# Expert rows gathered in tiles: the first product computed turned from copied weights, and a new order of work

## The reference

```python
x = x + L1_xcond(layernorm(x), ctx, ...)      # cross attention, 16 heads, layer 2 of the kernel
x = x + L1_ffn(layernorm(x), ...)             # layer 3, "sorted"
x = x + L2_xcond(ctx, layernorm(x), ...)      # local attention with a window, layer 4, "local"
...
# L1_ffn: 8 experts, each token goes to one
h = relu(einsum('td,edh->teh', tokens, W1) + b1[None])      # 128 -> 256
y = einsum('teh,ehd->ted', h, W2) + b2[None]                # 256 -> 128
out = take_along_axis(y, expert)[:, 0, :]; return out * max_prob
```

## Time and profile before

| | |
|---|---|
| runs, us | 961.96, 957.6, 962.65; median 961.96 |
| profiled execution | 961.87 us, span on the core 960.1 us |
| mean granted TensorE clock | 0.868 of full speed |
| busy share PE / DVE / ACT / POOL | 75% / 61% / 36% / 26% |
| chain that ended last | PE 48%, DVE 25%, POOL 8%, issue 8%, ACT 5%, DMA 4% |

### The profile page before, as it was taken

The page is one execution under the profiler, slowest core; times in us unless marked ns, Lnnn a source line. Parts: engine busy times, 40 slices in busy tenths (PEclk is TensorE's granted clock), DMA queues, the critical chain, the costliest instruction groups (busy, mean ns, idle before and its releaser), DMA issues.

```text
span 960.1 us, 13382 instructions
## 1 busy us (share of the span) xinstructions
PE 724.2 (75%) x3940; PEld 452.8 (47%) x3940; DVE 590.4 (61%) x2000; ACT 346.5 (36%) x582; POOL 254.2 (26%) x304
## 2 busy tenths in 40 slices
PE   2677874889984766675777459777867788789998
PEld 1223332889982222234656335655644233355554
DVE  6656647455455556553544558798777566586673
ACT  6255412645650552242121122122314456323221
POOL 2240267550664654112340431120111100000000
PEclk9979865899996895787987669979989899699999
DMA  6273022354643411611211000203011110000000
GB/s 177 62 249 112 17 77 91 118 174 133 189 135 85 112 48 30 204 70 53 81 46 42 23 0 1 74 1 80 1 50 50 50 50 1 0 1 12 12 12 11
DMA packets 71216, 65.65 MB, mean 68 GB/s; under 512 B 8996, under 2 KB 62941, under 8 KB 70634
## 3 DMA queue, kind: packets, MB, share of 16 engines
q1 hardware_dynamic: 53610, 48.14, 17.1%
q0 software_dynamic: 5120, 10.50, 3.7%
q10 hardware_dynamic: 12416, 6.16, 2.2%
HBM read 35.73 MB, written 22.94 MB: 61 GB/s over the span
## 4 chain that ended last, share of the span: by engine, by line
PE 48%; DVE 25%; POOL 8%; issue 8%; ACT 5%; DMA 4%; SPq 1%; DVEq 0%; ACTq 0%; POOLq 0%
PE psum_all L700 4%; PE psum_all L676 4%; DVE s_nmx L1340 4%; PE psum_all L678 3%; PE psum_all L805 3%; PE psum_all L893 3%; PE psum_all L657 3%; PE psum_all L787 3%; PE psum_all L789 3%; PE psum_all L909 2%; ACT s_hT L2102 2%; DVE s_x_normed L1237 2%; PE psum_all L775 2%; PE psum_all L613 2%; POOL routed_x L2426 2%
## 5 line engine op out<-in xcount | busy, mean ns | idle before, releaser
L2520 POOL TENSOR_SCALAR s_vare<-s_mv 128x4 f32<-128x4 f32 x40 | 11.6, 289 | 388.1 <-DVE s_mv L1229 378.8
L1340 DVE TENSOR_REDUCE s_nmx<-psum_all 128x4 f32<-128x308 f32 x192 | 83.2, 473 | 49.9 <-PE psum_all L657 46.3
L2102 ACT ACTIVATE s_hT<-psum_all 77x1024 f32<-77x1024 f32 x96 | 95.9, 1017 | 40.6 <-PE psum_all L678 40.5
L676 PE MATMUL psum_all<-s_t,s_ks 128*77 128x512 bf16 x192 | 84.1, 438 | 13.1 <-ACT s_hT L2102 9.6
L657 PE MATMUL psum_all<-s_ks,s_t 128*128 128x308 bf16 x192 | 59.6, 360 | 44.2 <-DVE s_nmx L1340 30.1
L678 PE MATMUL psum_all<-s_t,s_ks 128*77 128x512 bf16 x192 | 82.6, 430 | 0.0
L700 PE MATMUL psum_all<-s_hT,s_v 77*32 77x512 f32 x384 | 59.2, 690 | 26.1 <-ACT s_hT L2102 26.0
L2440 POOL DMA_INDIRECT s_w<-routed_y,s_cT x64 | 61.8, 966 | 56.1 <-issue 55.2
L2426 POOL DMA_INDIRECT routed_x<-s_x_normed,s_cT x64 | 62.4, 975 | 45.5 <-DVE s_cT L1541 27.2
L657 PEld LDWEIGHTS psum_all<-s_ks,s_t 128*128 128x128 bf16 x192 | 18.4, 103 | 99.1 <-DVE s_nmx L1340 65.8
L2199 ACT ACTIVATE s_hT<-psum_all,s_cols 128x128 f32<-128x128 f32 x188 | 51.1, 382 | 36.8 <-PE psum_all L893 32.7
(11 more groups left out here) (315 smaller groups left out, 1528.7 us busy)
## 6 DMA issues: line engine op xcount, KB each, us to landing
s_t<-q_parts SPq DMA_DIRECT2D x66, 128.0 KB, 2.9
routed_y<-s_hT ACTq DMA_DIRECT2D x22, 256.0 KB
s_ks<-s_att SPq DMA_DIRECT2D x72, 77.0 KB, 2.1
q_parts<-s_qparts SPq DMA_DIRECT2D x11, 384.0 KB, 2.3
s_arena<-in_w SPq DMA_DIRECT2D x2, 2048.0 KB, 10.7
s_h<-routed_x SPq DMA_DIRECT2D x48, 64.0 KB
s_x_normed<-routed_x SPq DMA_DIRECT2D x46, 64.0 KB
routed_x<-s_w SPq DMA_DIRECT2D x34, 64.0 KB, 1.5
```

The costliest lines, as they stand in the source:

```text
L676: pe.matmul(PS[0:SK, k + y, :], KS1[:, h, keys], T1[:, u % QS, h // HPG, :], start=True, stop=False)
L1340: read(job, dve.tensor_reduce(nmx[:, u % 2, i, HPG * g:HPG * g + HPG], PS[:, k, 0:HPG * SK].rearrange("p (h s) -> p h s", h=HPG), AX.X, AL ...
L2102: read(("S", L, b, p), nc.scalar.activation(Eexp[:, (PAIRS * u + p) % ES, :, :], PS[0:SK, k:k + 2, :], ACT.Exp))
```

## The change

- Inner rows turned: `sorted_hidden` on TensorE multiplies with a copy of the expert's W1 (`SW1`, in the place of `HSg`) as the stationary operand, so that its product comes out turned, in two halves of 128; there is no bias matmul. ScalarE adds the bias as a column (new columns `b1_3` in the table `cols`, chosen by a register) in eight ReLU activations a quad and writes `HTg` itself. `sorted_turn_hidden` and `sorted_copy` are gone.
- VectorE copies W1 of each tile (`sorted_first_weights`), ahead of the quad.
- `attn_out` of the last batch stands ahead of the tiles; the first two turnings of each half stand together; the values follow the next quad's inner rows; fronts, route, rank and local scores have new places; `local_add` of batches 0 and 1 moves from the end of the sorted layer into `local_layer`, behind `front_stats(L, 2)`.
- `PB` and its two helpers hold 128 columns instead of 384; `r_end` shares the memory of `tile_expert`.

TensorE:

```diff
             def sorted_hidden(L, h, q):
                 n = len(QUADS[L]) * h + q
                 have(("XT", L, h, q))
+                pe.wait_ge(s_rw1, R_STEPS + n + 1)
                 k = start(("SH", L, h, q), WIDE)
-                for i, t in enumerate(QUADS[L][q]):
-                    o = PS[:, k + i // 2, 256 * (i % 2):256 * (i % 2) + 256]
-                    pe.matmul(o, XST[:, n % 2, 128 * i:128 * i + 128], w1_rows[:, bass.ds(expert_at[h, t], 256)],
-                              start=True, stop=False)
-                    mm = pe.matmul(o, SEL[:, bass.ds(expert_at[h, t] // 2, 128)], PB[:, 0:256], start=False, stop=True)
+                for i in range(len(QUADS[L][q])):
+                    for c in range(2):
+                        a = 256 * i + 128 * c
+                        mm = pe.matmul(PS[:, k + a // 512, a % 512:a % 512 + 128], SW1[:, n % 2, a:a + 128],
+                                       XST[:, n % 2, 128 * i:128 * i + 128], start=True, stop=True)
                 finish(("SH", L, h, q), mm)
```

VectorE:

```diff
-            def sorted_copy(L, h, q):
...
+            def sorted_first_weights(L, h, q):
+
+                n, some = len(QUADS[L]) * h + q, QUADS[L][q]
                 if n >= 2:
-                    dve.wait_ge(*slots.is_made(("SY", L, (n - 2) // len(QUADS[L]), (n - 2) % len(QUADS[L]))))
...
+                    dve.wait_ge(*slots.is_made(("SH", L, (n - 2) // len(QUADS[L]), (n - 2) % len(QUADS[L]))))
+                dve.wait_ge(s_te, h + 1)
+                regs = r_regs[0:len(some)]
+                dve.reg_load(regs, tile_expert[0:1, h, some[0]:some[-1] + 1])
+                at = [dve.snap(r, min_val=0, max_val=(EXPERTS[L] - 1) * 256) for r in regs]
+                for i in range(len(some)):
+                    ins = dve.tensor_copy(SW1[:, n % 2, 256 * i:256 * i + 256],
+                                          w1[L][:, :, :].rearrange("p e h -> p (e h)")[:, bass.ds(at[i], 256)])
+                ins.then_inc(s_rw1, 1)
```

`local_layer` on VectorE, and ScalarE's inner rows:

```diff
                 sorted_add(L - 1, 1, range(0, TPB))
                 front_stats(L, 2)
+                local_add(L, 0)
+                local_add(L, 1)
                 front_stats(L + 1, 0)
                 front_apply(L, 2)
```

```diff
             def sorted_hidden(L, h, q):
-                n = len(QUADS[L]) * h + q
-                w = 256 * len(QUADS[L][q])
+                n, some = len(QUADS[L]) * h + q, QUADS[L][q]
                 k = made(("SH", L, h, q))
+                act.wait_ge(s_te, h + 1)
                 if n >= 2:
-                    act.wait_ge(*slots.is_made(("HT", L, (n - 2) // len(QUADS[L]), (n - 2) % len(QUADS[L]))))
-                read(("SH", L, h, q), nc.scalar.activation(HSg[:, n % 2, 0:w], PS[:, k:k + 2, :].rearrange("p a b -> p (a b)")[:, 0:w],
-                                                           ACT.Relu))
+                    act.wait_ge(*slots.is_made(("SY", L, (n - 2) // len(QUADS[L]), (n - 2) % len(QUADS[L]))))
+                regs = r_regs[0:len(some)]
+                act.reg_load(regs, tile_expert[0:1, h, some[0]:some[-1] + 1])
+                at = [act.snap(r, min_val=0, max_val=(EXPERTS[L] - 1) * 256) for r in regs]
+                first = COLS["b1_3"][0]
+                for i in range(len(some)):
+                    for c in range(2):
+                        a = 256 * i + 128 * c
+                        ins = nc.scalar.activation(HTg[:, n % 2, a:a + 128], PS[:, k + a // 512, a % 512:a % 512 + 128], ACT.Relu,
+                                                   bias=cols[:, first + c:first + 15 + c][:, bass.ds(at[i] // 128, 1)])
+                read(("SH", L, h, q), ins)
```

More of the change, by code:

```diff
@@ L1768, in sorted_layer @@
                 gauss_context()
[L1770 removed]
+                first(1, 2)
+                values(1, 0)
                 sorted_add(L, 0, range(0, TPB))
                 front_stats(L + 1, 0)
+                first(1, 3)
+                values(1, 1)
                 sorted_add(L, 0, range(TPB, 2 * TPB))
```

121 lines of the change are left out of this document (46 added, 75 removed).

## The result

The changed kernel takes 954.64 us (median of 20 executions) against 962.81 us for the kernel before beside it: ratio 0.9924, interval 0.9898 to 0.9951, about 7 us of gain (5 to 10) where 14 were forecast; the median still lies inside the range given, at its upper end (955). Two later comparisons on other chips gave 0.9908 (0.9864 to 0.9952) and 0.9871 (0.983 to 0.9911). The profiled execution took 952.14 us.

The account below looks back on a forecast made before the run. The prediction took one chain passed around TensorE, ScalarE and VectorE in fixed order, plus TensorE's register loads, as the bound; -2.0 - 2.3 + 0.5 - 12.8 + 2.6 = -14.0 us gave 948 us, range 943 to 955.

Parts of the forecast that it names:

- -2.0: First half of the sorted layer: the scatter of half 1 starts at 464.1 us, not 466.15; 2.0 us gained.
- -2.3: First turning of half 1: register loads done before the rows land at 478.4 us, so it starts then; 2.3 us gained.
- +0.5: Load of half 1's rows: the first gather now runs beside it; 0.5 us lost, between 0 and 1.
- -12.8: Second half, first turning to VectorE's last read: 29.8 us instead of 42.6; 12.8 us gained.
- +2.6: Last read to the local layer's front of batch 2: 18.0 us instead of 15.4, behind tanh and local add; 2.6 us lost.
- the layers follow one another: Behind the front of batch 2: what is gained reaches the end, with the distance unchanged at 419.4 us.
- Prices of the parts: Per quad: ReLUs 2.17 us, starting 0.69 us after the last matmul; weight copies 0.90 us, costing the scatter 0.
- Rival A: Slower hand-overs (3.5 us), copies holding the scatter (1.8), a second-half quad at 1.2 GHz (4): 957 us, chance 0.22.

Follow-up runs that it names:

- e_ranks_alone: The changed kernel with only ranks and slots of half 1 put ahead of values 1; ratio to the kernel before 0.9876.
- e_regs: The changed kernel with TensorE's four expert register loads a quad replaced by one, placed at the values; ratios to the kernel before 0.9865, 0.9809 and 0.9855.
- e_addback: The changed kernel with both local adds back at the end of VectorE's sorted layer; ratios to the kernel before 0.9971 and, repeated, 0.9904.
- e_regs_old: The kernel before with one register load of a quad's four tile experts instead of four, at the same place; ratio to the kernel before 0.9967.

## Why the forecast was half right

*Direction and mechanism: right.* The second turnings, their copies and hand-overs are gone; the halves shortened, and the end with them. The size was not. Term by term, each profile of the changed kernel against the profile of before beside it, in us:

| term of the sum | forecast | first pair | second pair |
|---|---|---|---|
| start of half 1 after the first turning ("-2.0", "-2.3") | -4.3 | -2.7 | -3.5 |
| load beside the gather ("+0.5") | +0.5 | in the row above | in the row above |
| second half ("-12.8") | -12.8 | -10.6 | -9.8 |
| last read to front 2 ("+2.6") | +2.6 | +4.6 | +4.0 |
| front 2 to the end ("the layers follow one another") | 0 | -1.3 | +4.7 |
| sum | -14.0 | -10.1 | -4.6 |

The runs put the gain at 7.3 us; that the mean of two pairs so far apart gives the same is luck.

*Prices of the parts: right.* ScalarE's ReLUs take 2.18 us and start 0.7 us after the inner rows' last matmul. The weight copies, 0.90 us, cost the scatter nothing. In the second profile:

```profile
471.80 0.96 POOL L2462 DMA_INDIRECT sorted_x<-s_x_normed,s_slot_of  x1 [0.30 <-issue]
472.05 1.00 DVE L1711 COPY s_arena<-s_w 128x256 f32 x4
473.06 0.96 POOL L2462 DMA_INDIRECT sorted_x<-s_x_normed,s_slot_of  x1 [0.30 <-issue]
```

With copies beside them the scatters behind the first keep 0.95 to 0.96 us and a pitch of 1.26 us, as the last one in the earlier trace rows; it is the copies that take 1.00 to 1.08 us there. The lock-out that the Trainium skill (SBUF — State Buffer, section "SBUF: two separate sides") states for such copies beside descriptor writing, priced at 1.8 us in the prediction, is not seen.

*"-2.0", scatter 23.5 us after the first turning: 25.4 in the first profile, 23.9 in the second.* In the first one the inner rows of quad 2 took 3.41 us, nearly all at 1.2 GHz, and the ranks stood behind values 1. e_ranks_alone shows that this term was not worth pricing closely: the turning of half 1 hangs on the context matmul as well.

*"-2.3", first turning of half 1: right from the scatter on.* 14.0 and 14.2 us after the scatter, against 14.3 in the layout; released by the load in both profiles. The 0.5 us for a gather beside this load don't show. What is late comes from the scatter.

*"-12.8", second half in 29.8 us: the step that failed.* It took 32.0 and 32.3 us, for two reasons. The first 1.0 us is in both profiles and is not the clock: from the start of values 0 to the turning of quad 2 the layout had 3.6 us (488.4 to 492.0), measured were 4.4 (490.57 to 494.96), with 1.96 us of idle time in front of the turning, the register loads. e_regs, without them, has no gap there. The other 1.2 and 1.5 us are a fall of the clock inside a half that I had laid out at 2.4 GHz from inner rows 1 on. In the first profile it lasts from 495.74 to 499.15 us, and inner rows 2 take 3.38 us, where the same 16 passes take 2.05 in the second profile; there the fall lies at the last values instead (507.47 to 510.88 us). The slow clock at the start costs nothing: it lasted until 488.91 us in the first profile, and the 32 passes of quads 0 and 1 took 6.11 us against 5.58 in the second and some 5.0 in my layout, but values 0 start 10.2 us after the first turning in both (10.0 in the layout), since TensorE then waits for ScalarE. The three profiles of e_regs say the same: its second half takes 28.3 us with 3.4 us at 1.2 GHz and 31.2 with 10.1, but 31.4 with 6.5, so the place of a fall counts and not its length alone. Rival A named this, "one quad of the second half runs at 1.2 GHz again", as one of three mishaps and at 4 us; the other two did not happen, and -7 lies between it and the forecast.

*"+2.6", last read to front 2 in 18.0 us: 20.0 and 19.3.* I took 8.1 us for the chain from the probabilities to the end of the second tanh from a stretch mostly at 2.4 GHz; in the first profile it takes 10.3 us and runs at 1.2 GHz until 526.46 us (the context product L842 alone takes 3.62 us). The traces bear the clock out: this chain takes 8.1 and 8.3 us with 1.4 and 1.2 us at 1.2 GHz (before), 9.6 with 6.1 (second profile), 10.3 with 7.6 (first). With the adds at their old place this stretch takes 22.3 and 22.8 us (e_addback, e_addback_b), so the moved adds did their part.

*"From there on the layers follow one another": a term put at nothing, wrong by up to 4.7 us.* I had set 2 us as the bound at which this falls. The two profiles of the changed kernel agree to 0.01 us for 15 us behind front 2 and part in two steps. Between the same two turned fronts, first profile above, second below:

```profile
547.44:559.90 12.46, 8.49 (x48) 6.68 (x49) 5.87 (x25) 4.12 (x7) 2.62 (x4) 0.88 0.01 1
546.29:561.55 15.26, 11.30 (x49) 8.64 (x49) 5.87 (x25) 4.11 (x7) 2.62 (x4) 0.71 0.00 1
674.24:833.31 159.07, 126.26 (x610) 62.92 (x609) 106.34 (x365) 71.06 (x87) 14.39 (x18) 0.88 0.10 30
675.84:837.76 161.92, 125.11 (x610) 62.06 (x609) 106.24 (x365) 71.00 (x87) 14.37 (x18) 0.88 0.10 30
```

The first step, 2.8 us, is more time at 1.2 GHz: TensorE is busy 2.8 us longer with the same work, and nothing else changes. The second, 2.9 us, comes at the same mean clock. Its first part is the place of a fall; the same scaled adds, read by VectorE from TensorE, in the two profiles:

```profile
681.47 1.13 DVE L1463 SCALAR_TENSOR_TENSOR s_h<-psum_all,s_combine,s_h 128x128 f32<-128x128 f32 x4 [0.54 <-PE psum_all L775]
684.33 1.13 DVE L1463 SCALAR_TENSOR_TENSOR s_h<-psum_all,s_combine,s_h 128x128 f32<-128x128 f32 x4 [1.81 <-PE psum_all L775]
```

In the second profile the clock has fallen on the very matmuls (L775) that VectorE waits for. Elsewhere the same number of slow microseconds meets work with slack. Both steps occur in other kernels: in the twelve profiles with 23.9 of the 30 us behind the front at half clock, front 2 to end is 420.8 to 423.6 us; in the other eight (18.8 to 24.7) it is 418.0 to 421.4. No run sets the clock, so what decides where it falls stays open, as do the worth of the new start and of the register loads in time (2.5 us, within the noise).

## What to carry to other kernels

When a kernel keeps its idle time and loses work, price its matmuls at both clocks, not at the one the old trace had in that place, and ask in each place whether another engine waits for them: here the same fall cost 1.2 us or more in one place and nothing in another. Filling the idle time raised the clock in the layer, but a gain in time couldn't be told from the noise. Removing a step from a chain and reordering the queues around it can be worthless each and worth 1% together; try the four corners, on one chip, before crediting either. When one release is made earlier, look which other one ends last (context matmul and register loads here), before pricing the next edit on it.

## What was not expected of the hardware

One kernel, e_regs, had in the same stretch 10.2 us at half clock in one profile and 20.3 in another, worth 3.1 us. And the same program spent equal time at half clock in a stretch of 160 us (mean clock 0.88 in both), yet took 2.9 us longer where a fall met matmuls that VectorE waited for. Four single register loads from memory part two turnings by 1.6 us after a turning of 1.1, some 0.6 to 0.7 us for each load as an estimate from this, while in e_regs_old one load of four at the same place shows no gap. And one program, the kernel before, takes 965 to 969 us on two chips and 1034 to 1041 us on three, nearly all of the difference before this layer.
